# The layer norm of the last stage with tokens on the partitions, its roots moved to GpSimd

## The reference

```python
x1 = x @ sw1.T + sb1;  x2 = x @ sw2.T + sb2           # 128 hidden
sh = ln(silu(x1) * x2, s_ln_g, s_ln_b)                # over the 128
shared_out = sh @ sw3.T + sb3                         # 256 per token
x_moe = x[index_b, index_t]                           # the picked tokens
shared_score, expert_scores = sigmoid(x_moe @ sg_w.T + sg_b), sigmoid(x_moe @ eg_w.T + eg_b)
top1 = argmax(expert_scores + exp_bias)
w = softmax([shared_score, expert_scores[top1]])
z = ln(silu(x_moe @ ew1[e].T + eb1) * (x_moe @ ew2[e].T + eb2), sel_ln_g, sel_ln_b)
expert_out = (z @ ew3[e].T + eb3)[top1]
out = shared_out, at the picked tokens shared_out * w[0] + expert_out * w[1]
return x + out
```

## Time and profile before

| what | value |
|---|---|
| median of 3 executions | 583.89 us (580.96 to 586.48) |
| the profiled execution's own time | 583.43 us |
| its span in the trace | 581.7 us, 17023 instructions |
| granted TensorE clock, mean | 0.993 |
| TensorE (PE) busy | 569.2 us, 98% |
| VectorE (DVE) | 409.2 us, 70% |
| ScalarE (ACT) | 262.7 us, 45% |
| GpSimd (POOL) | 177.6 us, 31% |
| chain of waits | PE 96%, issue 1%, DVE 1% |

### The profile page before, as it was taken

How to read it: one execution, slowest core, us unless ns; L and a number is a source line. 1 busy time by engine, 2 the same in 40 slices (tenths; PEclk the granted TensorE clock), 3 DMA queues, 4 the chain that set the end, 5 groups by cost and what they waited for, 6 DMA issues and landing times.

```text
span 581.7 us, 17023 instructions
## 1 busy us (share of the span) xinstructions
PE 569.2 (98%) x5107; PEld 501.2 (86%) x5108; DVE 409.2 (70%) x1093; ACT 262.7 (45%) x576; POOL 177.6 (31%) x529
## 2 busy tenths in 40 slices
PE   9999999999999999999999999899999998999995
PEld 5888888885889999999999999799999996866874
DVE  5969996767846686777577688755756554568766
ACT  6666757622344343435343343343435342546360
POOL 0270000000663435352524323335242500189000
PEclk9999999999999999999999999999999998999999
DMA  8712254101001223220000000000000000192322
GB/s 266 258 76 72 79 174 145 56 1 38 2 1 32 81 103 117 83 102 38 2 2 3 2 2 3 2 3 2 3 1 3 2 4 5 30 366 81 110 101 87
DMA packets 28479, 36.92 MB, mean 63 GB/s; under 512 B 4762, under 2 KB 24115, under 8 KB 28132
## 3 DMA queue, kind: packets, MB, share of 16 engines
q1 hardware_dynamic: 28292, 35.57, 18.6%
q0 software_dynamic: 96, 0.20, 0.1%
HBM read 27.30 MB, written 8.53 MB: 62 GB/s over the span
## 4 chain that ended last, share of the span: by engine, by line
PE 96%; issue 1%; DVE 1%; ACT 0%; POOL 0%; POOLq 0%; DVEq 0%
PE ps_hidden L1168 43%; PE ps_out L1196 42%; PE ps_hidden L598 4%; PE ps_hidden L647 1%; PE ps_out L618 1%; PE ps_turn L1202 1%; PE ps_out L1242 1%; PE ps_out L610 1%; PE ps_turn L631 1%; PE ps_small L631 1%; DVE X L788 1%; DVE ytmp L871 0%; PE ps_turn L1249 0%; PE ps_small L1246 0%; ACT hbuf L533 0%
## 5 line engine op out<-in xcount | busy, mean ns | idle before, releaser
L1196 PE MATMUL ps_out<-hbuf,W 128*128 128x242 f16 (+2 forms) x2304 | 250.7, 269 | 0.0
L1196 PEld LDWEIGHTS ps_out<-hbuf,W 128*128 (+1 forms) x2304 | 224.4, 98 | 18.8 <-issue 0.2
L1741 POOL COPY xs<-X 128x88 f16 x352 | 126.4, 408 | 288.5 <-PE ps_hidden L1168 179.2
L1038 ACT ACTIVATE h<-ps_hidden,b 128x242 f32<-128x242 f32 (+1 forms) x384 | 155.5, 465 | 78.8 <-PE ps_hidden L1168 78.8
L1168 PE MATMUL ps_hidden<-xs,W 128*128 128x242 f16 x1536 | 165.8, 269 | 2.1 <-issue 2.1
L1168 PEld LDWEIGHTS ps_hidden<-xs,W 128*128 x1536 | 150.4, 98 | 12.8 <-issue 2.9
L1347 DVE TENSOR_TENSOR hbuf<-h,hbuf 128x484 f16<-128x484 f32 (+2 forms) x192 | 129.8, 676 | 7.5
L1628 DVE SCALAR_TENSOR_TENSOR acc<-ytmp,wrow,acc 128x44 f32 (+1 forms) x352 | 65.8, 260 | 94.7 <-ACT ytmp L1129 90.5
L1345 DVE CAST hbuf<-h 128x484 f16<-128x484 f32 (+2 forms) x192 | 84.9, 442 | 17.8 <-ACT h L1038 16.9
L1168 PE MATMUL ps_hidden<-X,W 128*128 128x256 f16 (+1 forms) x768 | 90.3, 279 | 2.7 <-issue 2.7
L1168 PEld LDWEIGHTS ps_hidden<-X,W 128*128 128x128 f16 x768 | 75.5, 99 | 15.7 <-issue 3.8
(11 more groups left out here) (294 smaller groups left out, 305.3 us busy)
## 6 DMA issues: line engine op xcount, KB each, us to landing
stage<-in_ew SPq DMA_DIRECT2D x16, 512.0 KB, 3.8
stage<-in_xR SPq DMA_DIRECT2D x8, 512.0 KB, 3.9
moved_rows<-stage SPq DMA_DIRECT2D x8, 512.0 KB, 2.6
X<-moved_rows SPq DMA_DIRECT2D x8, 512.0 KB, 10.0
out_rows<-X SPq DMA_DIRECT2D x16, 256.0 KB, 2.2
W<-in_xT SPq DMA_DIRECT2D x7, 512.0 KB, 9.2
W<-in_fw SPq DMA_DIRECT2D x1, 2304.0 KB, 11.8
W<-in_sw SPq DMA_DIRECT2D x4, 256.0 KB, 3.4
```

What stands on the lines that cost most here:

```text
L1038: i = nc.scalar.activation(h32[:, j, k * size:(k + 1) * size], ps1[j][:, k * size:(k + 1) * size], ACT.Gelu_apprx_tanh, bias=b1[:, bass.ds ...
L1196: mm = pe.matmul(out, w2(e, wp, hb, db), h, start=(n == 0), stop=(n == 3 * HB - 1))
L1741: i = nc.gpsimd.tensor_copy(xs[:, parity, :, j * SEG:(j + 1) * SEG], X[:, :, bass.ds(cols[j], SEG)])
```

## The change

The centred product is made with tokens on the partitions: each block of 128 tokens of `ghl` is the stationary operand and `Cm` the moving one, 8 matmuls of 128 columns per step, into two banks in turn. ScalarE squares each of the four blocks in an activation that also sums its row (`accum_out`), so the variance matmuls go. Roots of steps 0 to 3 are made by GpSimd, the first 15 operations ahead of its last 16 column copies, the others behind them; `rows(k)` waits for them. The column numbers are loaded 16 at a time. ScalarE takes Sqrt with bias and scale in one instruction. Scoring moves from step 6 to step 5, the one-hot's transpose (now into `ps1[3]`) to the end of step 7, the pick ahead of `second(6)`; `gsecond` is cut in two around `second(7)`, and `mixed` around `rows(7)`.

```diff
             def square(k):
                 act.wait_ge(c_done, k + 1)
-                if k >= 2:
-                    act.wait_ge(var_mm, k - 1)
-                nc.scalar.activation(sq[:, k % 2, :], psy[0], ACT.Square).then_inc(sq_ready, 1)
+                for n in range(MG):
+                    i = nc.scalar.activation(sq[:, k % 2, n * P:(n + 1) * P], psy[k % 2][:, n * P:(n + 1) * P],
+                                             ACT.Square, accum_out=sums2[:, k * MG + n:k * MG + n + 1])
+                i.then_inc(sq_ready, 1)
...
             def root(q):
-                act.wait_ge(var_taken, q + 3)
-                nc.scalar.activation(tms, tms, ACT.Sqrt).then_inc(root_made, 1)
+                act.wait_ge(sq_ready, 2 * q + 6)
+                two = slice((2 * q + 4) * MG, (2 * q + 6) * MG)
+                nc.scalar.activation(roots2[:, two], sums2[:, two], ACT.Sqrt, bias=epss,
+                                     scale=WS * WS / FH).then_inc(root_made, 1)
...
                 if k == 5:
                     gsilu(0, 0)
                     gsilu(0, 1)
+                    score(0)
                 if k == 6:
                     gsilu(0, 2)
                     gsilu(0, 3)
-                    score(0)
                 if k == 7:
                     mix(0)
                     gsilu(0, 4)
+            root(0)
             square(NQ - 1)
-            root(0)
             gcentre(0, 0)
...
             def centre(k):
                 pe.wait_ge(g_ready, k + 1)
-                if k >= 1:
-                    pe.wait_ge(sq_ready, k)
-                else:
+                if k >= 2:
+                    pe.wait_ge(sq_ready, k - 1)
+                elif k == 0:
                     pe.wait_ge(late_done, 2)
-                for part in range(2):
-                    mm = pe.matmul(psy[0], Cm, ghl[:, k % GR, part, :], start=(part == 0), stop=(part == 1))
+                for n in range(MG):
+                    for part in range(2):
+                        mm = pe.matmul(psy[k % 2][:, n * P:(n + 1) * P], ghl[:, k % GR, part, n * P:(n + 1) * P], Cm,
+                                       start=(part == 0), stop=(part == 1))
                 mm.then_inc(c_done, 1)
-
-            def variance(k):
-                pe.wait_ge(sq_ready, k + 1)
-                if k >= 2:
-                    pe.wait_ge(var_taken, k // 2)
-                for n in range(MG):
-                    mm = pe.matmul(psy[1][:, k * MG + n:k * MG + n + 1], sq[:, k % 2, n * P:(n + 1) * P],
-                                   onesm[:, 0:1], start=True, stop=True)
-                mm.then_inc(var_mm, 1)
 
...
             def turn_hot(g):
                 pe.wait_ge(hot2_ready, g + 1)
-                pe.wait_ge(var_taken, NQ // 2)
-                pe.transpose(psy[1][0:FE, 0:P], roh, ident[:, :]).then_inc(hot_turned, 1)
+                pe.wait_ge(gg_made, g * 5 + 4)
+                pe.transpose(ps1[3][0:FE, 0:P], roh, ident[:, :]).then_inc(hot_turned, 1)
 
             def gcentre(g, n):
                 pe.wait_ge(gg_made, g * 5 + (4, 5, 5)[n])
+                if n == 0:
+                    pe.wait_ge(hot_taken, g + 1)
                 if n == 2:
                     pe.wait_ge(sq_ready, NQ)
                 j0, m = PARTS[n]
@@ -669,11 +670,13 @@
                 mm.then_inc(gvar_mm, 1)
 
             def pick(g):
-                pe.wait_ge(hot_taken, g + 1)
+                pe.wait_ge(sq_ready, NQ)
                 pe.matmul(psy[1][:, D:2 * D], ohT, ce8, start=True, stop=True).then_inc(pick_mm, 1)
 
-            def gsecond(g):
-                for j in range(NJ):
+            def gsecond(g, lo=0, hi=NJ):
+                if lo == 0:
+                    pe.wait_ge(gsq_ready, g * 3 + 2)
+                for j in range(lo, hi):
...
             for k in range(1, NQ):
                 first(k)
                 centre(k - 1)
-                if k >= 2:
-                    variance(k - 2)
                 if k >= 4:
                     second(k - 4)
                 if k == 5:
@@ -702,21 +703,20 @@
                     gfirst(0, 3)
                 if k == 7:
                     gfirst(0, 4)
+                    turn_hot(0)
             centre(NQ - 1)
-            variance(NQ - 2)
             second(4)
-            variance(NQ - 1)
             second(5)
             for n in range(3):
                 gcentre(0, n)
-            second(6)
-            second(7)
-            turn_hot(0)
-            gvariance(0)
             pe.wait_ge(w3s_in, 16)
             pe.wait_ge(ce8_in, 16)
             pick(0)
-            gsecond(0)
+            second(6)
+            gvariance(0)
+            gsecond(0, 0, 4)
+            second(7)
+            gsecond(0, 4, NJ)
...
             def late_roots(q):
                 two = slice(2 * q * MG, (2 * q + 2) * MG)
                 dve.wait_ge(root_made, q - 1)
-                link(nc.vector.reciprocal(rstd[:, two], tms))
+                link(nc.vector.reciprocal(rstd[:, two], roots2[:, two]))
 
             def rows(k):
                 dve.wait_ge(x_rows_in[k], 16)
                 dve.wait_ge(u_done, k + 1)
+                if k < 4:
+                    dve.wait_ge(var_taken, k // 2 + 1)
...
             def take_hot(g):
                 dve.wait_ge(hot_turned, g + 1)
-                nc.vector.tensor_copy(ohT, psy[1][0:FE, 0:P]).then_inc(hot_taken, 1)
+                nc.vector.tensor_copy(ohT, ps1[3][0:FE, 0:P]).then_inc(hot_taken, 1)
...
+            def picked(g):
                 dve.wait_ge(pick_mm, g + 1)
                 nc.vector.tensor_scalar(moe2, psy[1][:, D:2 * D], rm[:, 4:5], None, ALU.mult).then_inc(moe_step[1], 1)
-                for j in range(1, NJ):
+
+            def mixed(g, lo=0, hi=NJ):
+                if lo == 0:
+                    dve.wait_ge(gu_done, g * 5 + 1)
+                    nc.vector.scalar_tensor_tensor(moe, last_bank(0), rstdg[:, 0:1], moe, ALU.mult,
+                                                   ALU.add).then_inc(moe_step[0], 1)
+                for j in range(max(lo, 1), hi):
+                    if j == NJ - 1:
+                        dve.wait_ge(moe_step[1], g * 5 + 5)
+                        nc.vector.tensor_tensor(moe2, moe2, moe, ALU.add).then_inc(moe_step[0], 1)
                     if j % 2 == 0:
                         dve.wait_ge(gu_done, g * 5 + (j // 2 + 1))
+                    if j == NJ - 1:
+                        dve.wait_ge(moe_step[0], g * 5 + 5)
+                        nc.vector.scalar_tensor_tensor(moe, last_bank(j), rse[:, j - 1:j], moe2, ALU.mult,
+                                                       ALU.add).then_inc(moe_ready, 1)
...
                     choose(0)
-            late_roots_in(2)
+            take_hot(0)
             rows(3)
             ggated(0, 4)
             weights(0)
             late_roots(2)
             rows(4)
-            late_roots_in(3)
             rows(5)
+            picked(0)
             late_roots(3)
             rows(6)
+            groots_in(0)
+            groots(0)
+            mixed(0, 0, 4)
             rows(7)
-            groots_in(0)
-            take_hot(0)
-            groots(0)
-            mixed(0)
+            mixed(0, 4, NJ)
...
-            def gather(g):
+            def gather(g, meanwhile=None):
                 nc.gpsimd.indirect_dma_start(
                     out=xg, out_offset=None, in_=a["xR"],
                     in_offset=bass.IndirectOffsetOnAxis(ap=gid[:, g:g + 1], axis=0)).then_inc(xg_in, 16)
-                for at in range(0, P, 8):
-                    pool.load(regs, ctab[0:1, g * P + at:g * P + at + 8])
+                for at in range(0, P, 16):
+                    if at == 112 and meanwhile is not None:
+                        meanwhile()
+                    pool.load(regs, ctab[0:1, g * P + at:g * P + at + 16])
                     cols = [pool.snap(x, min_val=0, max_val=COLS - 1) for x in regs]
-                    for j in range(8):
+                    for j in range(16):
                         i = nc.gpsimd.tensor_copy(cgT[:, :, at + j:at + j + 1], column(cols[j]))
                 i.then_inc(cg_pool, 1)
+
+            def roots(q):
+                taken = [q * 14]
+
+                def link(i):
+                    taken[0] += 1
+                    i.then_inc(root_step, 1)
+                    pool.wait_ge(root_step, taken[0])
+
+                pool.wait_ge(sq_ready, 2 * q + 2)
+                two = slice(2 * q * MG, (2 * q + 2) * MG)
+                out = rstd[:, two]
+                link(nc.gpsimd.tensor_scalar(tms, sums2[:, two], 1.0 / FH, EPS, ALU.mult, ALU.add))
+                link(nc.gpsimd.tensor_scalar(out.bitcast(I32), tms.bitcast(I32), -0.5, MAGIC, ALU.mult, ALU.add))
+                for n in range(3):
+                    link(nc.gpsimd.tensor_tensor(qms, out, out, ALU.mult))
+                    link(nc.gpsimd.tensor_tensor(qms, qms, tms, ALU.mult))
```

(56 more changed lines are left out.)

2 lines of the change are left out of this document (1 added, 1 removed).

## The result

The changed kernel takes 588.03 us in the median of 12 executions (584.43 to 590.34), the kernel before 584.34 in the same job: ratio 1.0078, 95% interval 1.0055 to 1.0101. That is slower, but by less than 1%. A later job with the unaltered kernel gave 1.0048 (1.0022 to 1.0074). The profiled execution took 584.43 us for a span of 582.3, the quickest of its twelve, so its trace shows the smaller part of the loss.

What follows compares the result with a forecast made beforehand. TensorE was taken to bound the stage up to the last group, VectorE the end after it. The router 4.5 us later and the stretch behind it 1.6 shorter gave +2.9, hence 586.8 us, range 582 to 591.

Steps and rivals of the forecast that it cites:

- Centre step: TensorE's centred product as eight matmuls of 128 columns: 0.62 us, between bounds of 0.43 (columns alone) and 0.79.
- TensorE's own saving: In the stage, eight variance steps go (-6.3 us) and eight centre steps grow (+1.5): a gain of 4.8 us.
- A square with its sums: ScalarE's four 128-column squares with row sums per step: 1.3 us, bounds 0.85 and 2.0 (sum instruction at most 0.19, L527).
- The 0.8 us of waits at three centres: TensorE waiting on ScalarE's loop in steps 1 to 3, about 0.27 us at each centre, 0.8 in all.
- `roots(0)`: GpSimd's 15 linked operations before the last 16 copies: start 533.4, 4.9 us plus 0.75 and 0.7, end 539.75.
- first use: In GpSimd's roots(0), the first tensor_tensor of the kernel costs extra: 0.75 us taken, 0 to 1.1.
- The stop by VectorE's two-input work: GpSimd stands still during VectorE's two-SBUF-input work; about 0.7 us of g_low(4) falls into roots(0).
- the step at eight registers: GpSimd register loads: eight take 0.57 us, eleven 1.25, so 16 would cost 1.25 or more and win nothing.
- The second wait of 2.1: TensorE before the router: second(1) ends at 542.9, but the last copies hold the router until 545.0.
- From the router to the last addition: Stretch behind the router: 35.6 us, -1.6 against 37.23 before, with gated(7) 14.1 after the router.
- the wait for take_hot: In VectorE's queue behind the router, a wait of 0.7 us for turn_hot, part of 4.8 us of waits.
- the early pick: With split gsecond, saves TensorE 0.7 us idle and VectorE a 1.27 stall; rows(7) amid mixed gives it back.

Runs made afterwards that it cites:

- the first filler run: Changed kernel plus 20 matmuls of 512 columns with unused results between centre(4) and second(1): 587.77 us, ratio 1.0046.
- The run without the moves: Changed kernel with roots of steps 0 to 3 on VectorE and scoring, transpose, pick, gsecond and additions as in the kernel before: 582.06 us, ratio 0.9949.
- the narrow loads: Changed kernel with the column numbers loaded 8 registers at a time again instead of 16: 587.12 us, ratio 1.0051.
- one Newton round: Changed kernel with one Newton round of three in GpSimd's roots, 7 operations instead of 15 ahead of the last copies: 585.59 us, ratio 0.9999.
- the hybrid: Changed kernel with roots(0) on VectorE and roots(1) on GpSimd behind its last copy: 580.96 us, ratio 0.9935.

## Why the prediction was right

The forecast was 586.8 us (+2.9) in a range of 582 to 591; measured 588.03 (+3.7), and +2.0 in the later job. The main mechanism held: GpSimd's serial roots in front of the last copies held rows(0), second(1) and the router. The single terms, each as distance from first(1) and against the forecast in brackets:

- Centre step 0.45 us (0.62), as in this row of the changed kernel's chain of waits:

```profile
548.27 0.45 PE ps_out L617 x8
```

   So the loads hide almost entirely and the lower bound holds: 0.056 per load and multiply. By the Trainium skill (TensorE: Matmul & The Clock Gate, "Back-to-back issue gap") a pair takes about 81 ns, which would have made 0.65; this trace doesn't agree. TensorE's own saving was 6.2 us, not 4.8, so the sum had that term too small.
- A square with its sums 1.02 us (1.3). ScalarE's timeline shows the sum as an instruction of its own, the tiny one that I had bounded by L527:

```profile
520.96 0.28 ACT L507 ACTIVATE W<-ps_out 128x128 f32<-128x128 f32 x1
521.14 0.20 ACT L507 ACTIVATION_READ_ACCUMULATOR W<-ps_out 128x1 f32 x1
...
521.98 0.65 ACT L515 ACTIVATE W<-W 128x512 f16<-128x512 f32 x1
```

   The 0.8 us of waits at three centres didn't come; TensorE reached second(1) after 16.9 (18.2).
- `roots(0)` started after 15.4 (14.0) and took 4.2 (6.35), so it ended after 19.6 (20.4). Two errors cancelled, a start 1.4 too early and a length 2.15 too long, and that they did is luck. The operations took 0.28 (0.325), and no first use was dear. The stop by VectorE's two-input work that I had put into the roots came ahead of them: steps are 3.1 us long now instead of 3.8, so c_low(6) and g_low(4) both fell among the copies. That is the likely reason why the roots, ahead of copy 112, could only start 1.4 us later than that copy's place in the kernel before.
- second(1) after 21.5 (21.9); its wait was 4.6 (3.7), for TensorE was there earlier. The load of 16 cost 1.055 (1.25): the step at eight registers that I read from rows 6 isn't there. The last 16 copies took 3.57 (3.6). The router after 24.6 (25.4), +3.6 (+4.5).
- The second wait of 2.1 was only 0.38 in the trace, because second(1) ran at the lower clock and used it up. In the first filler run, where second(1) runs at the upper level, the wait before the router is 1.64.
- From the router to the last addition 35.9 (35.6 by the chain's start of the router, 35.8 by the timeline's, which is 0.17 earlier), with gated(7) 14.1 behind the router (14.1 or 14.3). TensorE's 1.50 before second(4) is the wait for take_hot that I had counted in VectorE's queue. That the early pick would give nothing in the end was forecast, but for another reason (rows(7) in the middle of the additions). The run without the moves shows no difference beyond chance; which reason it is, no run shows.

Together the stage grew by 2.2 in the first trace (+2.9). What the prediction lacked altogether is the clock behind a pause that it had itself foreseen: 2.7 us between two executions of the same program. It may be what makes +3.7 of the trace's +2.2, but the later job's +2.0 leaves that open. That the total came so near is thus partly luck: TensorE's saving was larger than forecast, the router's delay smaller, and the clock no part of the sum.

## What to carry to other kernels

Work off a busy engine is only cheap where it lands behind everything that others wait for in the new queue: 15 such operations ahead of the last copies are the difference between a ratio of 1.005 to 1.008 (588 us) and one of 0.995 (581.8), 15 behind them cost nothing that could be measured. Ask of each wait that a move creates not only who waits for the result, but what stands behind it in the same queue, here 16 copies and the router. And count a long chain of tiny linked operations by its links: eight links of 0.28 us were 2.1 us of kernel. When two traces are compared, compare the clock of the same stretch first: 1.7 us between the ends of two of these runs were nothing else.

## What the runs showed of the hardware

- A pause of 4.6 us of TensorE was followed by its lower clock level in both traces of the changed kernel and in that with the narrow loads, one of 2.48 us (one Newton round) was not. In the second trace the level stayed low (0.57 over the stretch from 540 to 550 us) though TensorE was busy 9.62 of 10 us of it. With all roots on VectorE it was 0.69 from 566 to 571.5 us, with TensorE busy throughout and no pause since the 1.50 us that ended at 558.07.
- A GpSimd register load takes 0.566 us for 8 and 1.055 for 16 on the same line of the kernel, so per register nearly the same. The load of eleven at L1736, at an address computed in a loop, takes 1.25, so the number of registers isn't all that counts.
- GpSimd's small operations take 0.20 us, one input or two, and 0.28 linked. Beside VectorE's two-input c_low and g_low, one behind the other, one took 1.75. It is in GpSimd's timeline of the hybrid, in roots(1):

```profile
538.27 0.20 POOL L974 TENSOR_SCALAR stage<-stage 128x8 f32<-128x8 f32 x1
538.55 1.75 POOL L975 TENSOR_TENSOR stage<-stage 128x8 f32<-128x8 f32 x1
```

- A row sum on ScalarE is an instruction of its own: it starts 0.16 to 0.18 us behind its activation of 128 columns, and the next activation 0.09 behind it, 0.25 per pair.
